# Expert outputs made and sent half by half, with four result buffers and earlier reads of the results, in a fused two-block kernel

## The reference

```python
def _L1_ffn_ref(x, Wg, W1, b1, W2, b2):        # D = 128, F = 512, E = 8, K = 2
    logits = jnp.einsum('bsd,de->bse', x, Wg)
    P = jax.nn.softmax(logits, axis=-1)
    _, topk_idx = jax.lax.top_k(P, K)
    mask = jax.nn.one_hot(topk_idx, E, dtype=x.dtype).sum(-2)
    P_topk = P * mask
    P_norm = P_topk / (P_topk.sum(axis=-1, keepdims=True) + EPS)
    h = jax.nn.gelu(jnp.einsum('bsd,edf->ebsf', x, W1) + b1[:, None, None, :], approximate=False)
    y_e = jnp.einsum('ebsf,efd->ebsd', h, W2) + b2[:, None, None, :]
    return jnp.einsum('ebsd,bse->bsd', y_e, P_norm)
...
x = x + s * _silu(_L1_ffn_ref(xn, ...))
```

## Time and profile before

| | |
|---|---|
| median of three runs | 450.25 us |
| the profiled execution's own time | 446.94 us |
| its span in the trace | 445.2 us |
| TensorE busy | 409.0 us (92%) |
| VectorE busy | 284.5 us (64%) |
| ScalarE busy | 213.8 us (48%) |
| GpSimd busy | 155.7 us (35%) |
| mean granted TensorE clock | 0.997 |

### The profile page before, as it was taken

One profiled execution on the slowest core, in us unless ns is written; L12 is line 12 of the kernel. 1 busy time (PEld: TensorE's weight loads), 2 busy tenths in 40 slices (PEclk: granted clock), 3 DMA queues, 4 the chain that ended last, 5 costly groups with the idle time before them and its releaser, 6 DMA issues. The chain is left out here.

```text
span 445.2 us, 9851 instructions
## 1 busy us (share of the span) xinstructions
PE 409.0 (92%) x2944; PEld 344.6 (77%) x2944; DVE 284.5 (64%) x1137; ACT 213.8 (48%) x525; POOL 155.7 (35%) x215
## 2 busy tenths in 40 slices
PE   7699989999999999999988999888999999999882
PEld 7579777878869779787767779777899999998630
DVE  4889889888887878878867657412233343433327
ACT  3364555565554545543424353333555555555412
POOL 6340015013233340443433011534454555455510
PEclk9999999999999999999999999999999999999998
DMA  7449411154064330131222223321222222222576
GB/s 181 123 114 166 57 40 42 50 170 135 13 192 122 81 79 25 47 83 53 75 54 61 66 51 80 101 80 54 68 71 67 78 71 71 61 77 68 169 275 193
DMA packets 64210, 40.80 MB, mean 92 GB/s; under 512 B 18340, under 2 KB 57128, under 8 KB 64168
## 3 DMA queue, kind: packets, MB, share of 16 engines
q1 hardware_dynamic: 59472, 31.27, 28.2%
q0 software_dynamic: 4352, 8.99, 6.1%
q10 hardware_dynamic: 344, 0.03, 0.1%
HBM read 21.78 MB, written 18.48 MB: 90 GB/s over the span
## 5 line engine op out<-in xcount | busy, mean ns | idle before, releaser
L694 POOL DMA_INDIRECT routed<-send,slot x64 | 64.5, 1008 | 129.1 <-DMA routed<-send,slot 57.5
L703 POOL DMA_INDIRECT results<-nat,y_to x72 | 69.8, 969 | 89.0 <-DVE nat L1638 65.4
L1029 PE MATMUL psA<-xuT,w_all 128*128 128x256 f32 x288 | 68.9, 381 | 3.5 <-ACT h1T L1239 3.2
L1239 ACT ACTIVATE h1T<-psA,b1T 128x256 f32<-128x256 f32 x144 | 63.1, 473 | 12.0 <-PE psB L1052 7.5
L1029 PEld LDWEIGHTS psA<-xuT,w_all 128*128 128x128 f32 x288 | 50.6, 190 | 11.5 <-issue 2.9
L1041 PE MATMUL psC<-w_all,h1T 128*128 128x128 f32 x464 | 56.7, 275 | 1.0 <-DVE nat L1622 1.0
L1610 DVE TENSOR_SCALAR xu<-ring 128x256 f32 (+1 forms) x38 | 11.2, 295 | 71.2 <-DMA ring<-routed 67.0
L1041 PEld LDWEIGHTS psC<-w_all,h1T 128*128 128x128 f32 x464 | 54.1, 192 | 1.3 <-ACT h1T L1239 1.1
L1230 ACT ACTIVATE xuT<-psB 128x256 f32<-128x256 f32 x37 | 14.2, 383 | 61.6 <-PE psB L1019 45.8
L843 PE MATMUL psB<-xnT,w_l 128*128 128x512 f32 x64 | 34.3, 618 | 0.0
L1170 ACT ACTIVATE hg0T<-psB,b1T 128x512 f32<-128x512 f32 x32 | 22.0, 688 | 22.9 <-PE psB L845 22.8
(11 more groups left out here) (289 smaller groups left out, 851.8 us busy)
## 6 DMA issues: line engine op xcount, KB each, us to landing
ring<-routed SPq DMA_DIRECT2D x38, 130.0 KB
inv<-inv_room SPq DMA_DIRECT2D x8, 512.0 KB
w_all<-results SPq DMA_DIRECT2D x15, 256.0 KB, 4.1
routed<-ring SPq DMA_DIRECT2D x24, 130.0 KB, 6.7
n_room<-nT SPq DMA_DIRECT2D x8, 256.0 KB
w_all<-in_L_ffn_W_dram SPq DMA_DIRECT2D x1, 2048.0 KB
out_dram<-x_all SPq DMA_DIRECT2D x8, 256.0 KB, 2.3
results<-nat,y_to POOLq DMA_INDIRECT x72
```

Source lines behind the costliest of these rows:

```text
L694: pool.indirect_dma_start(routed[:, :], bass.IndirectOffsetOnAxis(ap=slot[par][:, c, t:t + 1], axis=0), send[par][:, c, t, :], None).then_ ...
L703: pool.indirect_dma_start(results[:, :], bass.IndirectOffsetOnAxis(ap=y_to[:, par, a:a + 1], axis=0), yw[:, par, a, :], None).then_inc(S[f ...
L1029: last = mm(psA[:, j // 2, (j % 2) * UNIT:(j % 2 + 1) * UNIT], w1_all[:, e, j * P:(j + 1) * P], xuT[:, :], start=True, stop=True)
L1239: f(h1T[:, j, :], psA[:, j // 2, (j % 2) * UNIT:(j % 2 + 1) * UNIT], ACT.Gelu, bias=b1T[:, n:n + 1]).then_inc(S["gelu_ready"], 1)
```

## The change

It has these parts.

1. `out` goes half by half: four products of half 0, then four of half 1. Half 0 signals `half_ps`. Chunk k is told free (`h1_free`) by the product of half 1.
2. VectorE takes each half from PSUM on its own, with one instruction that scales and adds (L1698 of the changed kernel), the bias times the weight being made before in `yb` (L1690). Places, weights and `yb` are made before the wait for the products. Each half signals GpSimd, which sends it at once.
3. There are four `yw` and not two, so `results_of` of unit u waits for the results of unit u-4 and not u-2. Rounds of GpSimd's loop have four units; where the number of units is no multiple of four, spare sends fill it up. Here it is 36.
4. VectorE keeps, after each of the first seven groups of the routing, how many rows experts 6 and 7 have (`held`), and makes of it a table `reach`: the number of units that must have landed before that group's lower, or higher, results are complete.
5. SyncE makes no unneeded loads. It reads `reach` and loads the results group by group, each once the units it needs have landed.
6. Group 0's two results are added on VectorE in SBUF. TensorE puts the first of its sums, the lower one of group 1, ahead of the last unit's output. The silus are written over the lower results in `w1_all`, so they wait for no buffer. VectorE finishes groups 0, 1, 2-3, 4-5, 6, 7, two groups by one instruction where a pair stands; after group 0 it writes the places of the spare sends.

The core of the diff:

```diff
+ENDS = ((0, 1), (1, 2), (2, 4), (4, 6), (6, 7), (7, 8))
+YBUFS = 4
...
-        def other_units(eng, bounds, hid, out):
+        def other_units(eng, bounds, hid, out, between=lambda: None):
...
+            between()
             out(bounds[E] - 1, E - 1, None)
...
-            load_unit(bounds[E], 0)
-            load_unit(bounds[E] + 1, 0)
-            wait_on(sp, "unit_in", (bounds[E] + 2) * 16)
+            wait_on(sp, "unit_in", bounds[E] * 16)
...
-            wait_on(sp, "y_landed", bounds[E - 1])
-            load_results(0, res_lower, lower_in)
-            sp.wait_ge(all_landed, 1)
-            load_results(1, res_higher, res_in)
+            sp.wait_ge(reach_ready, 1)
+            for g in range(groups - 2):
+                wait_on(sp, "y_landed", units_for(g, 0))
+                load_results(0, g, res_lower, lower_in)
+            wait_on(sp, "y_landed", units_for(0, 1))
+            load_results(1, 0, res_higher, res_in)
+            wait_on(sp, "y_landed", bounds[E - 1])
+            for g in range(groups - 2, groups):
+                load_results(0, g, res_lower, lower_in)
+            for g in range(1, groups - 1):
+                wait_on(sp, "y_landed", units_for(g, 1))
+                load_results(1, g, res_higher, res_in)
+            wait_on(sp, "y_landed", bounds[E])
+            load_results(1, groups - 1, res_higher, res_in)
...
             def out(u, f, e):
-                wait_on(pe, "yb_ready", u)
-                for k in range(JF):
-                    wait_on(pe, "gelu_ready", u * JF + k + 1)
-                    for a in range(HALVES):
+                wait_on(pe, "yw_ready", u * HALVES)
+                for a in range(HALVES):
+                    for k in range(JF):
+                        if a == 0:
+                            wait_on(pe, "gelu_ready", u * JF + k + 1)
                         last = mm(psC[:, a, 0:D], h1T[:, k, a * P:(a + 1) * P],
                                   w2_all[:, f * JF + k, :], start=(k == 0), stop=(k == JF - 1))
-                    last.then_inc(S["h1_free"], 1)
+                        if a == HALVES - 1:
+                            last.then_inc(S["h1_free"], 1)
+                    if a == 0:
+                        last.then_inc(S["half_ps"], 1)
...
+                for a in range(HALVES):
+                    last = v.tensor_scalar(yb[:, a, :], b2_all[:, f, :], y_wt[:, a:a + 1], None, ALU.mult)
+                last.then_inc(S["yb_ready"], 1)
                 wait_on(dve, "yb_ready", u + 1)
                 for a in range(HALVES):
-                    last = v.tensor_scalar(yw[:, mine, a, :], yb[:, a:a + 1, :], y_wt[:, a:a + 1],
-                                           None, ALU.mult)
-                last.then_inc(S["yw_ready"], 1)
+                    if a == 0 and by_halves:
+                        wait_on(dve, "half_ps", u + 2 - FIRST_ALL)
+                    else:
+                        wait_on(dve, "h1_free", (u + 1) * JF)
+                    v.scalar_tensor_tensor(yw[:, mine, a, :], ps[:, a:a + 1, :], y_wt[:, a:a + 1], yb[:, a:a + 1, :],
+                                           ALU.mult, ALU.add).then_inc(S["yw_ready"], 1)
```

More of the change, by code:

```diff
@@ L275, in two_block_kernel @@
         table = sb("table", [1, 2 * E + 2], I32)
+        held = sb("held", [1, groups - 1, 2])
+        held_i = sb("held_i", [1, groups - 1, 2], I32)
+        reach_f = sb("reach_f", [1, groups - 1, 2])
+        reach = sb("reach", [1, (groups - 1) * 2], I32)
         kT = sb("kT", [P, GW])
@@ L297, in two_block_kernel, with mix1 @@
         h1T = sb("h1T", [P, JF, UNIT])
-        yw = nat[:, 0:2 * HALVES, :].rearrange("p (i a) d -> p i a d", i=2)
-        yb = nat[:, 2 * HALVES:3 * HALVES, :]
-        y_to = sb("y_to", [P, 2, HALVES], U32)
+        yw = nat[:, 0:YBUFS * HALVES, :].rearrange("p (i a) d -> p i a d", i=YBUFS)
+        yb = sb("yb", [P, HALVES, D])
+        y_to = sb("y_to", [P, YBUFS, HALVES], U32)
+        spare = sb("spare", [P, YBUFS, HALVES], I32)
         silu_first = sb("silu_first", [P, 1])
         y_wt = sb("y_wt", [P, HALVES])
-        th1 = [hg0T[:, i, :].rearrange("p (t d) -> p t d", t=TILES) for i in range(2)]
-        mix2 = [hg0T[:, 2 + i, :].rearrange("p (t d) -> p t d", t=TILES) for i in range(2)]
+        def mix1(first, end):
+            return w1_all[:, first:end, :].rearrange("p g (t d) -> p (g t) d", d=D)
         res_lower = [w1_all[:, g, :].rearrange("p (a d) -> p a d", d=D) for g in range(groups - 1)] + [nT[0][:, :, :]]
@@ L316, in sum_ps_of @@
         def sum_ps_of(g):
-            return (psD, psA, psB, psC)[g // 2][:, g % 2, :]
+            return (psD, psA, psB, psC)[(g - 1) // 2][:, (g - 1) % 2, :]
         def tiles(ps, n=TILES):
@@ L715, in unit_work @@
                 elif what == "out":
[L716 removed]
+                    send_results(k, k % YBUFS)
             first_pass(pool, work, unit_work)
[L719 removed]
+            send_results(FIRST_ALL - 1, (FIRST_ALL - 1) % YBUFS)
             pool.wait_ge(table_ready, 1)
[L721 to L728 removed]
+            rounds_end = pool.value_load(table[0:1, 2 * E + 1:2 * E + 2], min_val=FIRST_ALL,
+                                         max_val=MAX_UNITS + YBUFS - 1)
+            assert FIRST_ALL % YBUFS == 0
+            with pool.Fori(FIRST_ALL, rounds_end, YBUFS) as u:
+                for buf in range(YBUFS):
+                    send_results(u + buf if buf else u, buf)
+            pool.wait_ge(S[f"y_sent{YBUFS - 1}"], rounds_end * (16 * HALVES // YBUFS))
+            pool.sem_inc(S["y_landed"], 1)
         def load_small(act):
@@ L1079, in _, with lower @@
             first_pass(pe, work, unit_work)
-            other_units(pe, bounds, hid, out)
-            for g in range(groups):
+            def lower(g):
                 pe.wait_ge(lower_in[g], 16)
-                if g == 0:
+                if g == 1:
                     wait_on(pe, "s1_ready", groups)
-                elif g == 4:
+                elif g == 5:
                     pe.wait_ge(S["xuT_ready"], bounds[E] + 1)
-                elif g == 6:
-                    wait_on(pe, "yb_ready", bounds[E])
+                elif g == 7:
+                    wait_on(pe, "yw_ready", bounds[E] * HALVES)
                 mm(sum_ps_of(g), ident[:, :], res_lower[g], start=True, stop=False)
-            for g in range(groups):
+            other_units(pe, bounds, hid, out, lambda: lower(1))
+            for g in range(2, groups):
+                lower(g)
+            for g in range(1, groups):
                 pe.wait_ge(res_in[g], 16)
@@ L1262, in _ @@
             f(silu_first[:, :], b1T[:, 0:1], ACT.Silu)
-            for g in range(groups):
-                act.wait_ge(S["sum_ps"], g + 1)
-                if g >= 2:
-                    act.wait_ge(S["mix_ready"], g - 1)
-                f(th1[g % 2][:, :, :], tiles(sum_ps_of(g)), ACT.Silu).then_inc(S["silu1_ready"], 1)
+            act.wait_ge(sum_sb, 1)
+            f(mix1(0, 1), mix1(0, 1), ACT.Silu).then_inc(S["silu1_ready"], 1)
+            for g in range(1, groups):
+                act.wait_ge(S["sum_ps"], g)
+                f(w1_all[:, g, :], sum_ps_of(g), ACT.Silu).then_inc(S["silu1_ready"], 1)
         @block.vector
@@ L1544, in work @@
                     v.tensor_copy(slot[par][:, :, :], slot_f[:, :, :]).then_inc(S["slots_ready"], 1)
+                    if g < groups - 1:
+                        link(v.tensor_copy(held[:, g, :], filled[0:1, E - 2:E]))
                     if g == groups - 2:
```

120 lines of the change are left out of this document (70 added, 50 removed).

## The result

The changed kernel took 458.17 us (median of four runs, 457.15 to 458.99), the kernel before beside it 449.07 (446.58 to 451.49): ratio 1.0223, 95% interval 1.0176 to 1.0270. The forecast was 457 and "slower". Its profiled execution took 457.15 us with a span of 454.9, against 446.94 and 445.2: +10.2 us, where the prediction's sum was +8.3. The direction and the larger terms were right.

A forecast was written before the change was run, and what follows sets the result against it. TensorE bounds the loops, then the end bounds the time; +14.8 (loops) + 0.5 (routing) − 7.0 (end) = +8.3 us, 455.2 against the profiled 446.94, or 457 from the middle 448.6; range 452.5 to 463.

The forecast's parts named there:

- Part 2: VectorE and GpSimd in the loops: their added instructions and sends cost and gain nothing, since TensorE waits for ScalarE alone.
- Part 1: Output products half by half in the loops: late Gelus stall TensorE, period 4.32 us for 3.75, +14.8 us over 26 periods.
- unit 6: Unit already made half by half in the kernel before: first Gelu 1.38 us after its output, period 4.32, taken as model.
- the low bound: Loops: first Gelu at 1.32 instead of 1.38 and the branches' own time hidden in the wait; period 4.25, +13.0 us.
- the high bound: Loops: Gelus stay 0.45 us apart, so the second ends 0.08 later; period 4.40, +16.9 us.
- Part 3: Routing: copies and small steps added on VectorE during the first pass, mostly covered; 0 to +1.5, taken as +0.5 us.
- Part 4: The end, after unit 34's output starts: 23.3 us instead of 30.3, bound by TensorE's and VectorE's queues; −7.0 us.
- T: The start of unit 34's output, from which the prediction counts times in the end of the kernel.
- The end did not pay for the loops: Rival at the end: only unit 35's landing bounds it, T+17.5, −12.8, net +2.5, 451 us, no change; chance 0.11.
- The Gelus were not in time for TensorE: Rival in the loops: second Gelu done within 1.79 us, no stall, only the end counts, −6.5, 442 us; chance 0.03.
- The reads were not late: Rival at the end: SyncE's reads hold higher loads until the last landing, first sum at T+11.7, 459 us; chance 0.10.
- The clock did not fall: Rival in the loops: idle of 0.6 us per period brings the clock to 1.2 GHz, about +97, 555 us; chance 0.02.

The follow-up runs named there:

- the chunk-by-chunk version: The changed kernel with the loops' output products back in the order of before, both halves of each chunk in turn; 454.65 us, ratio 1.0124.
- three traces of one group of runs: Changed kernel, old product order: with VectorE's old hand-over, 442.03 us; with sends waiting for a later hidden layer, 441.39; that with last sums interleaved, 441.32.
- the spaced version: The chunk-by-chunk version, with each loop unit's second send waiting until its first has landed; 466.87 us, ratio 1.0386.
- the later sends: The chunk-by-chunk version, with GpSimd waiting before a unit's sends for ScalarE's `xuT` of the unit three numbers on; 446.91 us, ratio 0.9962.
- the version with the wait between the sends: The chunk-by-chunk version, with GpSimd's wait for the landing of the unit before put between a unit's two sends; 450.58 us, one run.

## Why the prediction was right, and where it was wrong

**Part 2, "Nothing for either", is the step that failed.** It looked at how busy VectorE and GpSimd are, and at who waits for their results. By both measures it was right: nobody in the loops waits for them. But a result handed over earlier is also sent earlier. In the kernel before the two sends start 0.4 to 1.6 and 1.7 to 3.1 us after an output's start, so that what follows the second meets almost no Gelu (three first Gelus are 0.05 to 0.13 late). With the early hand-over, in the chunk-by-chunk version, the second send mostly starts at 0.55 to 0.58, and the third or the fourth Gelu waits until 1.5 to 1.65 us after it: 12.2 us in 26 periods. In the changed kernel itself the second mostly starts within 0.3 us of the output's start, and only the first Gelu is hit, from 1.32 to between 1.34 and 1.65, in 12 of the 26 periods (in two more the second Gelu is): 2.5 us. The half-by-half order hides the rest, since its Gelus are late anyway. Because of this overlap the two causes don't add: 13.3 and 12.2 apart, 15.9 together. It is also why taking the order back gave only 3.5 us, and why the kernel as a whole looked as if Part 1 alone explained it. Had only the total been compared (457 said, 458.17 measured), the fault would never have shown.

**Part 1, the order: right in its mechanism, a little too large.** Forecast 4.32 a period and +14.8, from unit 6. Undisturbed it is 4.259 and +13.3, near the low bound, 4.25: the first Gelu comes at 1.32, as 0.65 plus six passes gives, and not at unit 6's 1.38, whose extra was its own. The four Gelus take 1.57, as in unit 6, so the high bound's spacing of 0.45 did not come. By chance the hold fills the difference and more, to 4.357.

**Part 3, the routing**: +0.5 said, +0.3 measured up to unit 8's output, the step ahead of that unit included. One pair of traces can't size it: versions with the same routing reach unit 8's output anywhere from 316.02 to 320.06.

**Part 4, the end: right**, −6.5 for −7.0. The six lower sums run without gap, the first higher sum is at T+9.7 (9.6 said), VectorE's group 1 at T+11.4 (11.4), its last instruction ends at T+20.9 (20.6), and the write takes 2.85 for 2.7. The pairs' instructions take 1.22 to 1.23 us (1.23). One sum waited 0.58 for its load, in VectorE's shadow. Without any landing to wait for the end is 23.7, which excludes the landing as its bound.

**The rivals.** The end did not pay for the loops: 23.8, not 17.5. The Gelus were not in time for TensorE. The reads were not late: the first higher sum started at T+9.7 and not at 11.7. The clock did not fall: 1.00 in both windows of the loops, with idle times of 0.26 to 0.59 us ahead of the hidden layer in each period. The Trainium skill (TensorE: Matmul & The Clock Gate, section on a second failure mode, PSUM-queue cycling) tells of a bf16 kernel whose clock went back and forth at short idles between groups of products. If that held here, the clock would fall too; with these gaps between float32 products the trace shows nothing of it.

**What stays open.** It is shown that late news of TensorE's products is the loss that the order doesn't explain, that it follows the second of two sends 1.27 us apart, that it is gone without sends, and that moving or parting the sends lessens or removes it in traces that have it. Why the chip does so isn't shown, nor why three traces of one group of runs have no hold. The record of updates differs there even ahead of the loops: in the first 300 us these three traces keep 4372 to 4407 semaphore updates, all others 3647 to 3749. So the hold may hang together with how a trace is recorded, or with another state of the chip, and not only with the kernel; every time here is of an execution that was also profiled, so no run can tell. Nor was a version tried that keeps the half-by-half order and has a second `h1T`, which alone could take the order's price away.

## What to carry to other kernels

Before reordering products for an earlier consumer, list what each product's end sets free, not only what it completes: with one buffer for `h1T`, the order that completes half a result early frees its first chunk three products late, and the engine that was never idle pays in every round. When an edit makes a result ready earlier, follow it to the transfer it starts and look at what that transfer now lies beside. And take an edit apart even if the total comes out as forecast: here the same edits, less the order and with one wait ahead of the sends, make 441.4 us, 1.25% below the kernel before, where together they make it 2.2% slower. And measure versions that you want to compare in one group of runs: the share of that one wait stays open for want of it.

## What the runs showed of the hardware

- **A hold after GpSimd's second indirect send, in most traces.** Where two such sends of 0.97 us start 1.27 us apart, TensorE's semaphore updates that fall due about 0.6 to 1.5 us after the second one's start (in the spaced version from 0.4) mostly come late, and the instructions of ScalarE and VectorE that wait for them mostly begin 1.5 to 1.65 us after it: 361.19 to 362.68 in the changed kernel, 346.14 to 347.75 in the chunk-by-chunk one, 330.10 to 331.71 with the later sends, where the latest begin 1.86 us after it. The starts of the products themselves run on. The hold is no fixed window. In the version with the wait between the sends, Gelus due 0.58 to 0.72 us after the second send are late in all eight units that have them; there and in the chunk-by-chunk version, of 26 Gelus due 0.95 to 1.1 us after it 10 are on time; in the changed kernel the first Gelu, due 1.25 us after it, is late in some units (361.11) and on time in others (330.91). The first send of the two shows no such hold: in seven units of the kernel before (317.52 to 339.92) a Gelu starts on time 1.1 us after it. Nor does a send that starts 1.67 us or more after the one ahead, in the last periods of the version with the wait between. In three traces of one group of runs there is no hold at all: all 208 of TensorE's updates in the 26 periods are recorded on time, against 115 to 164 of 182 to 208 in the traces that have it. The Trainium skill (Perfetto Trace Analysis, section on an instruction's lifecycle) says that the time in which a semaphore's update travels lies outside the bar that a profile draws; by that rule a wait can end late though the bar it waits for ended on time, and the trace agrees: the bar at 345.56 has no gap, and the wait for it ends 0.65 us late.
- **When a chunk of `h1T` comes free sets the period in steps:** after product 2, 4 or 5 the first Gelu starts 0.65, 1.10 or 1.32 us after the output, and the period is 3.73, 4.04 or 4.26 us. TensorE's eight hidden passes start about 0.9 us after a delayed first Gelu (362.68 to 363.57).
